# A selective-scan block and a dequantised projection on one core: the last operand of each half's sums moves to VectorE, the statistics are cut into pieces, and three engines get another order in a chunk's border pairs

## The chip, the core and the metric

The kernel runs on one core of a Trainium2 chip. A core has a matrix engine (TensorE, PE in the profile), a vector engine (VectorE, DVE), a scalar engine (ScalarE, ACT), a general one (GpSimd, POOL) and a DMA-issuing queue (SyncE, SP). Each runs its own instruction stream in program order, and they meet at semaphores. The metric is the device time of one execution in microseconds (us).

## What is computed

For 4096 rows of 1024 numbers:

```
n  = layernorm(x)                                   # eps 1e-5
xi, z = split(n @ in_proj_w)                        # 1024 -> 2 * 2048
xc = silu(conv_b + sum_k conv_w[k] * shift(xi, k))  # 4 taps along the rows
p  = xc @ x_proj_w.T                                # 64 + 16 + 16 columns
dt = softplus(rmsnorm(p[:64]) @ dt_proj_w.T + dt_bias);  B, C = rmsnorm(p[64:80]), rmsnorm(p[80:96])
h[t] = exp(dt[t] * A) * h[t-1] + dt[t] * B[t] * xc[t]      # 16 states for each of 2048 channels
y[t] = sum over the 16 states of h[t] * C[t]
x2 = x + ((y + D * xc) * silu(z)) @ out_proj_w.T
out = x2 + layernorm(x2) @ W.T + bias               # W = scale * (code - 128)
```

## The kernel before

**Tiling.** The rows are cut into 16 chunks (c) of T = 256. The 2048 channels are 16 tiles of 128 partitions, taken two at a time: 8 pairs (j = 0 to 7). One step handles pair j of chunk c, S = 8c + j, so there are 128 steps. Beside the scan of chunk c a step holds one eighth of four other stages: the input projection, convolution and x-projection of chunk c+1, the output projection of chunk c-1 and the dequantised projection (ffn) of chunk c-2. Once in a chunk, around its border, two groups of 16 transposes of normalised rows are made: those of chunk c+2 for the input projection (`norm1`, last pair, j = 7) and those of chunk c-2 for the ffn (`norm2`, first pair, j = 0). Each is a chain: VectorE takes `bn_stats` of four blocks and `bn_aggr`, ScalarE turns them into a scale and a shift and writes two normalised row blocks into `xrow`, TensorE transposes four groups of four, and ScalarE copies each group out of PSUM.

**The scan of a pair.** A step has 16 units (two states each). For a unit ScalarE keeps the last state (`copy`, L1057) and writes two exponentials (L1061) into a PSUM bank `hb`; GpSimd has written dt * B * x for four states into `dbx` (L486); VectorE runs the scan in place (`scan(u)`, L1342) and multiplies by C (`product(u)`, L1290). GpSimd then adds the two halves of each pair of products (`half`, L494, eight groups k = 0 to 7 in a step), and TensorE sums the two remaining operands of each group into a PSUM bank by multiplying with the identity (`group(k)`, L574, two matmuls of 256 columns each). Groups 0 to 3 go to the bank `ys0` (channel tile a = 0), groups 4 to 7 to `ys1` (a = 1). When a tile's four groups are in, VectorE multiplies by the gate (`y_gate`, L1301) and raises `y_ready`. The gate of tile 0 stands after `product(9)` of its own step; that of tile 1 is called `late_y` and stands in the next step, after `product(1)`.

**What shares the banks.** `ys1` also receives the x-projection (`x_proj`, L604) and the dt projection (L624): `x_proj` in step S waits for `y_ready` of tile 1 of step S-1 (2S of them). `ys0` also receives the z projection (L614), whose second half waits for tile 0's gate. `g1` takes the output projection (L767, in four parts, `out_proj(0)` to `(3)`) and the ffn (L689) in turn, each behind VectorE's addition of the other (L1272: `add_out`, `add_ffn`). `gx` takes the input projection (L594) and all border transposes (L581).

**What sets the order.** Nothing is scheduled by a planner: every engine's order in a step is the order in which the code calls its pieces. On TensorE a middle pair is ffn, groups 6 and 7 of the step before, out(0), x_proj, out(1), group 0, x_in(0), group 1, x_in(1), group 2, out(2), group 3, dt, out(3), z(1), group 4, z(0), group 5.

Of the kernel before, what the change touches and what calls it, by code (L numbers as in the profile page):

```python
# [86 lines left out]
def build_program(nc, x, win, wout, wf_codes, wf_scales, ffn_bias, xproj, dtw_in, convw_in, convb_in,  # L87
                  alog_in, dparam_in, lnw_in, out):
    ctx = ExitStack()
    with ctx:  # L90
# [14 lines left out]
        def dsem(name):  # L105
# [108 lines left out]
        conv, scans, hcs, y_ready = sem("conv"), sem("scans"), sem("hcs"), sem("y_ready")  # L214
        xp_add, o_add, f_add = sem("xp_add"), sem("o_add"), sem("f_add")
        rms_red, l1_dve, l1_stats, l2_dve, l2_stats, aggr_go = (sem("rms_red"), sem("l1_dve"), sem("l1_stats"),
                                                                sem("l2_dve"), sem("l2_stats"), sem("aggr_go"))
# [226 lines left out]
        def _(pool):  # L444
# [122 lines left out]
        def _(pe):  # L567
            def group_sum(SG, k):
# [4 lines left out]
                for i in range(2):  # L573
                    mm = nc.tensor.matmul(ys[a][:, 0:T], ident[:], half[:, k % 4, i * T:(i + 1) * T],  # L574
                                          start=False, stop=(q == NQ - 1 and i == 1), skip_group_check=True)
# [87 lines left out]
            def iteration(st, c):  # L663
                def step(j):
# [52 lines left out]
                    def norm2(i):  # L717
                        if not (first and st.ffn):
                            return
# [71 lines left out]
                    if first and st.ffn or last and st.norm1:  # L791
# [10 lines left out]
                        norm1(3)  # L802
                    else:
                        out_proj(0)
                        x_proj()
                    out_proj(1)
                    if not (first and st.ffn or last and st.norm1):
                        group(0)
# [5 lines left out]
                    out_proj(2)  # L814
                    group(3)
                    dt_proj()
# [72 lines left out]
        def _(act):  # L889
# [144 lines left out]
            def iteration(st, c):  # L1034
                def step(j):
# [72 lines left out]
                    def norm2(i):  # L1108
                        if first and st.ffn:
                            if i == 0:  # L1110
                                act.wait_ge(f_mm, after(PAIRS * (c - 2)))
                            norm_evac(x2nT, 4 * (c - 2), i, gx, l2_tr, l2_evac)
# [47 lines left out]
                    norm2(0)  # L1160
                    norm1(0)
                    unit(4)
                    first_skip_term()
                    norm2(1)
                    norm1(1)
                    unit(5)
                    norm2(2)
                    norm1(2)
                    unit(6)
                    norm2(3)  # L1170
                    norm1(3)
                    unit(7)
                    rms_square()
                    unit(8)
                    rms_apply()
                    unit(9)
                    unit(10)
                    unit(11)
                    ss_out()
                    unit(12)  # L1180
                    x_taps()
# [5 lines left out]
                    norm1_start()  # L1187
                    norm1_row(0)
                    unit(15)
                    norm1_row(1)  # L1190
# [23 lines left out]
        def _(dve):  # L1214
            def stats(rows, bst, mv, mid, done, n):
                for tt in range(TT):
                    for h in range(2):
                        ins = nc.vector.bn_stats(bst[:, tt, 6 * h:6 * h + 6], rows(tt, h))  # L1218
                ins.then_inc(mid, 1)
                dve.wait_ge(mid, after(n))  # L1220
                dve.sem_inc(aggr_go, 1)
# [3 lines left out]

            def norm1_stats(chunk):
# [289 lines left out]
```

## Time and profile before

| what | value |
|---|---|
| median of 3 runs | 4703.04 us (4701.97 to 4705.4) |
| the profiled execution | 4697.21 us |
| its span, from the first to the last instruction | 4695.4 us |
| first scan / first scan of the last pair, from the span's start | 128.08 / 4535.14 us |
| PE, DVE, POOL, ACT busy, share of the span | 95%, 89%, 86%, 75% |
| a steady chunk (chunks 3 to 13) | 279.55 to 279.90 us |

A step's length is taken here from one `scan(0)` on VectorE to the next one. In chunk 8 the eight steps are, by these starts, 40.16, 33.20, 33.20, 33.20, 33.20, 33.20, 34.43 and 39.29 us. The idle time in square brackets in a row of the timeline is the engine's time without work just before the row, with the instruction that ended it.

### The profile page before, as it was taken

The numbers are of one execution on the slowest core, as the hardware profiler recorded it, in microseconds if no ns is written. First come the engines' busy times: TensorE is split into PE (matmuls) and PEld (weight loads), VectorE is DVE, ScalarE is ACT, GpSimd is POOL, SyncE is SP. The second block draws the span as 40 slices with busy tenths as digits, with TensorE's granted clock in tenths as the row PEclk, the third lists the DMA queues.
The fourth block names the chain that finished last, engine by engine and source line by source line (L and its number), as shares of the span: only waits on it lengthen the run. The fifth ranks groups of instructions, "written<-read, shape, count | busy, mean of one in ns | idle before, by whom it ended". The sixth has DMA issues, their size and how long they took to land.

```text
span 4695.4 us, 80181 instructions
## 1 busy us (share of the span) xinstructions
PE 4448.9 (95%) x26656; PEld 4049.0 (86%) x26656; DVE 4160.0 (89%) x5745; ACT 3542.4 (75%) x8848; POOL 4039.2 (86%) x2942
## 2 busy tenths in 40 slices
PE   7788989999999999999999999999999999999889
PEld 6567879989898998989989898998989889898779
DVE  3898989989899998989989899998989989899981
ACT  3777787877778787777877878787787777778760
POOL 0898989989898998989989898998989899899990
PEclk9889999999999999999999999999999999999999
DMA  7324243353434435343353534334353443434232
GB/s 255 130 79 161 99 159 139 114 186 133 173 129 161 145 138 175 124 178 128 123 188 123 177 137 165 137 128 173 138 180 120 145 165 129 165 127 155 90 115 94
DMA packets 160285, 678.56 MB, mean 145 GB/s; under 512 B 21120, under 2 KB 30080, under 8 KB 110720
## 3 DMA queue, kind: packets, MB, share of 16 engines
q1 hardware_dynamic: 141440, 639.88, 39.0%
q10 hardware_dynamic: 18432, 33.56, 1.9%
q8 instruction: 212, 3.47, 0.3%
q14 instruction: 201, 1.65, 0.1%
HBM read 618.32 MB, written 55.05 MB: 143 GB/s over the span
## 4 chain that ended last, share of the span: by engine, by line
PE 59%; DVE 20%; POOL 7%; issue 6%; ACT 5%; DMA 1%; SPq 0%; DVEq 0%; POOLq 0%; ACTq 0%
PE g L767 13%; PE gx L594 13%; PE ys L574 12%; DVE hb L1342 11%; PE ys L614 9%; PE g L689 4%; POOL dbx L486 4%; DVE hc L1290 4%; DVE gx L1238 2%; POOL half L494 2%; PE ys L604 2%; DVE bst L1218 2%; PE gx L581 2%; ACT hb L1061 1%; PE hb L853 1%
## 5 line engine op out<-in xcount | busy, mean ns | idle before, releaser
L1342 DVE TENSOR_TENSOR_SCAN hb<-hb,dbx 128x512 f32<-128x512 f32 x2048 | 2498.0, 1220 | 108.0 <-ACT hb L1061 84.4
L486 POOL TENSOR_TENSOR dbx<-dtx,bb 128x1024 f32<-128x1024 f32 x1024 | 2421.0, 2364 | 60.1 <-DVE hb L1342 34.9
L1061 ACT ACTIVATE hb<-dt,a_neg 128x256 f32<-128x256 f32 x4096 | 1789.5, 468 | 66.3
L494 POOL TENSOR_TENSOR half<-hc 128x512 f32<-128x512 f32 x1024 | 1303.1, 1273 | 135.4 <-DVE hc L1290 120.4
L1290 DVE TENSOR_TENSOR hc<-hb,cb 128x512 f32<-128x512 f32 x2048 | 1378.9, 673 | 0.0
L574 PE MATMUL ys<-half,ident 128*128 128x256 f32 x4096 | 1073.2, 389 | 133.4 <-POOL half L494 119.2
L574 PEld LDWEIGHTS ys<-half,ident 128*128 128x128 f32 x4096 | 757.2, 194 | 254.3 <-POOL half L494 151.3
L767 PEld LDWEIGHTS g<-wo,ybuf 128*128 128x128 f32 x7680 | 954.0, 198 | 20.2 <-issue 1.3
L767 PE MATMUL g<-wo,ybuf 128*128 128x128 f32 x7680 | 966.7, 281 | 0.6 <-issue 0.6
L614 PE MATMUL ys<-xnT,wz 128*128 128x256 f32 x4096 | 928.8, 380 | 1.6 <-DVE ybuf L1301 1.6
L594 PE MATMUL gx<-xnT,wx 128*128 128x256 f32 x3968 | 904.5, 381 | 4.3 <-DMA wx<-in_win 2.6
L1057 ACT COPY hstate<-hb 128x2 f32<-128x2 f32 x2044 | 319.3, 156 | 757.7 <-DVE hc L1290 754.5
L614 PEld LDWEIGHTS ys<-xnT,wz 128*128 128x128 f32 x4096 | 770.6, 191 | 103.1 <-DVE ybuf L1301 2.8
L594 PEld LDWEIGHTS gx<-xnT,wx 128*128 128x128 f32 x3968 | 756.9, 192 | 108.5 <-DMA wx<-in_win 3.0
L689 PEld LDWEIGHTS g<-wf,x2nT 128*128 128x128 f32 x3552 | 414.1, 192 | 5.7
L689 PE MATMUL g<-wf,x2nT 128*128 128x128 f32 x3552 | 414.5, 275 | 0.0
L1301 DVE TENSOR_TENSOR ybuf<-ys,gate 128x256 f32<-128x256 f32 x256 | 107.0, 418 | 237.8 <-PE ys L574 237.6
L1238 DVE SCALAR_TENSOR_TENSOR gx<-xpre,convw,gx 128x256 f32<-128x256 f32 x744 | 302.0, 482 | 13.8 <-ACT gx L942 13.8
L512 POOL TENSOR_TENSOR dtx<-dt,xcs 128x2 f32<-128x2 f32 x128 | 25.3, 198 | 282.7 <-ACT dt L992 176.8
L604 PE MATMUL ys<-xprojw,xcn 128*128 128x96 f32 x1024 | 152.0, 298 | 26.6 <-ACT xcn L951 23.5
L604 PEld LDWEIGHTS ys<-xprojw,xcn 128*128 128x128 f32 x1024 | 143.2, 215 | 33.9 <-issue 21.5
L1067 ACT ACT_TABLE_LOAD x128 | 164.2, 1283 | 2.3
(105 smaller groups left out, 2766.1 us busy)
## 6 DMA issues: line engine op xcount, KB each, us to landing
wz<-in_win SPq DMA_DIRECT2D x128, 1024.0 KB, 4.8
wx<-in_win SPq DMA_DIRECT2D x124, 1024.0 KB, 4.8
wo<-in_wout SPq DMA_DIRECT2D x123, 1024.0 KB, 4.9
wf<-wf_scratch SPq DMA_DIRECT2D x113, 512.0 KB, 3.2
xc_scratch<-xcn ACTq DMA_DIRECT2D x128, 256.0 KB, 2.1
xcs<-xc_scratch SPq DMA_DIRECT2D x128, 256.0 KB, 5.0
bb<-bc_scratch SPq DMA_DIRECT2D x64, 512.0 KB, 7.5
cb<-bc_scratch SPq DMA_DIRECT2D x64, 512.0 KB, 6.7
```

The lines of the kernel that those rows point to most:

```text
L486: nc.gpsimd.tensor_tensor(dbx[:, k % 2, :].rearrange("p (n t) -> p n t", n=NQ), dtx[:, S % 2, a, :].unsqueeze(1).to_broadcast([P, NQ, T]), ...
L494: nc.gpsimd.tensor_tensor(half[:, k % 4, :], hc[:, k % 2, 0:HALF], hc[:, k % 2, HALF:GW], ALU.add).then_inc(halves, 1)
L574: mm = nc.tensor.matmul(ys[a][:, 0:T], ident[:], half[:, k % 4, i * T:(i + 1) * T], start=False, stop=(q == NQ - 1 and i == 1), skip_group ...
L594: mm = nc.tensor.matmul(pair_bank(q)[:, a * T:(a + 1) * T], pair_weights(q)[:, kk, a * P:(a + 1) * P], xnT[:, chunk % 2, kk, :], start=(kk ...
L604: mm = nc.tensor.matmul(ys[1][:, tt * E:(tt + 1) * E], xcn[:, a * T + tt * P:a * T + (tt + 1) * P], xprojw[:, 2 * (q % PAIRS) + a, :], sta ...
L614: mm = nc.tensor.matmul(ys[0][:, a * T:(a + 1) * T], wz[:, kk, a * P:(a + 1) * P], xnT[:, q // PAIRS % 2, kk, :], start=(kk == 0), stop=(k ...
L689: mm = nc.tensor.matmul(g1[:, tt * P:(tt + 1) * P], x2nT[:, kk, tt * P:(tt + 1) * P], wf[:, kk, :], start=(kk == 0), stop=(kk == KH - 1))
L767: mm = nc.tensor.matmul(g1[:, tt * P:(tt + 1) * P], ybuf[:, (1 - st.parity) * PAIRS + kt // 2, (kt % 2) * T + tt * P:(kt % 2) * T + (tt + ...
L1061: ins = nc.scalar.activation(h[:, m * T:(m + 1) * T], dt[:, j % 2, a, :], ACT.Exp, scale=a_neg[:, ds((2 * j + a) * N + 2 * v + m, 1)])
L1238: nc.vector.scalar_tensor_tensor(bank[:, a * T:(a + 1) * T], xpre[:, a, tap:tap + T], convw[:, ds((2 * jq + a) * KC + tap, 1)], bank[:, a ...
L1290: nc.vector.tensor_tensor(hc[:, k % 2, w * UW:(w + 1) * UW], hb[u % 4][:], cb[:, n:n + 2, :].rearrange("p n t -> p (n t)"), ALU.mult).then ...
L1342: nc.vector.tensor_tensor_scan(h[:], h[:], dbx[:, k % 2, w * UW:(w + 1) * UW], 0.0, ALU.mult, ALU.add).then_inc(scans, 1)
```

## The change

- **The last operand of a half.** TensorE's groups 3 and 7 have one matmul in place of two. A new VectorE step, `last_sum`, adds the other operand from SBUF onto the PSUM bank, and the gate waits for it (semaphore `summed`). It waits for the group's matmul. GpSimd waits for `y_ready` before it writes groups 3 and 7 anew.
- **Where VectorE has the gates.** `late_sum` stands where `late_y` stood, and `late_y` is behind `scan(3)`. Likewise for tile 0: `last_sum` stands where the gate stood and the gate is behind `scan(11)`; in the last pair `last_sum` is behind `scan(12)` and the gate behind `product(11)`.
- **Statistics in pieces.** One `bn_stats` for `norm1` in each of pairs 1 to 4, with `bn_aggr` in pair 5; for `norm2` one each in pairs 5 and 6 and two in pair 7, with `bn_aggr` there. Before: four and `bn_aggr` in pair 6, and four and `bn_aggr` in pair 7.
- **The first pair.** TensorE does all of the output projection first, then the transposes, in `gx` and `g1` by turns, the dt projection, group 3 and the whole input projection. ScalarE writes the two normalised row blocks after units 5 and 6 and copies the transposes out before units 8 to 11; its work on the convolution (`x_taps`) stands after unit 14. VectorE's `add_out` stands after `product(7)` and its taps after `product(13)`.
- **Pairs 6 and 7.** ScalarE normalises the rows of `norm1` after units 8 to 10 of pair 6 (before: after units 14 and 15). TensorE has group 3 ahead of out(2) in pair 7.

VectorE around the gate of tile 1 in a middle pair, before (`SCALAR_TENSOR_TENSOR hb` is a scan, `hc` a product, `x2<-g1` is `add_ffn`, `ybuf<-ys1` is `late_y`):

```order
L1272 TENSOR_TENSOR x2<-g1,x2 128x2x128
L1342 SCALAR_TENSOR_TENSOR hb2<-hb2,dbx 128x512
L1290 TENSOR_TENSOR hc<-hb1,cb 128x512
L1301 TENSOR_TENSOR ybuf<-ys1,gate 128x256
L1342 SCALAR_TENSOR_TENSOR hb3<-hb3,dbx 128x512
L1290 TENSOR_TENSOR hc<-hb2,cb 128x512
```

The same place now, where `ys1<-ys1,half` is the new sum:

```order
L1310 TENSOR_TENSOR x2<-g1,x2 128x2x128
L1392 SCALAR_TENSOR_TENSOR hb2<-hb2,dbx 128x512
L1332 TENSOR_TENSOR hc<-hb1,cb 128x512
L1341 TENSOR_TENSOR ys1<-ys1,half 128x256
L1392 SCALAR_TENSOR_TENSOR hb3<-hb3,dbx 128x512
L1351 TENSOR_TENSOR ybuf<-ys1,gate 128x256
L1332 TENSOR_TENSOR hc<-hb2,cb 128x512
```

One instruction is new, and the gate of tile 1 is one scan and one sum later in the row.

TensorE in the first pair before, behind groups 6 and 7 (`ys0` or `ys1<-half` are groups, `gx<-ident` transposes, `g1<-wo` the output projection, `ys1<-xprojw` x_proj, `gx<-xnT` x_in, `ys1<-ssmT` dt):

```order
L581 MATMUL gx<-ident,xrow 128x128 x4
L604 MATMUL ys1<-xprojw,xcn 128x96 x4
L581 MATMUL gx<-ident,xrow 128x128 x4
L767 MATMUL g1<-wo,ybuf 128x128 x8
L581 MATMUL gx<-ident,xrow 128x128 x4
L574 MATMUL ys0<-half,ident 128x256 x2
L581 MATMUL gx<-ident,xrow 128x128 x4
L767 MATMUL g1<-wo,ybuf 128x128 x8
L594 MATMUL gx<-xnT,wx 128x256 x8
L574 MATMUL ys0<-half,ident 128x256 x2
L594 MATMUL gx<-xnT,wx 128x256 x8
```

The same stretch now, from x_proj on:

```order
L609 MATMUL ys1<-xprojw,xcn 128x96 x4
L773 MATMUL g1<-wo,ybuf 128x128 x8
L579 MATMUL ys0<-half,ident 128x256 x2
L773 MATMUL g1<-wo,ybuf 128x128 x8
L579 MATMUL ys0<-half,ident 128x256 x2
L773 MATMUL g1<-wo,ybuf 128x128 x8
L586 MATMUL gx<-ident,xrow 128x128 x4
L586 MATMUL g1<-ident,xrow 128x128 x4
L579 MATMUL ys0<-half,ident 128x256 x2
L586 MATMUL gx<-ident,xrow 128x128 x4
L586 MATMUL g1<-ident,xrow 128x128 x4
L629 MATMUL ys1<-ssmT,dtw 128x256 x2
```

The transposes moved behind all of the output projection and the input projection behind them.

The diff, cut to its core:

```diff
@@ POOL
             def group_sum(S, k):
                 pool.wait_ge(sum_mm, after(8 * S + k - 3))
+                if k % NQ == NQ - 1:
+                    pool.wait_ge(y_ready, after(2 * S + k // NQ))
@@ PE
             def group_sum(SG, k):
-                for i in range(2):
+                for i in range(1 if q == NQ - 1 else 2):
...
                     def norm2(i):
+                        pe.wait_ge(l2_ready, after(2 * (c - 2) + i // 2 + 1))
                         if i == 0:
                             pe.wait_ge(sx_act, after(xs_done))
-                            pe.wait_ge(l2_ready, after(2 * (c - 1)))
-                        else:
-                            pe.wait_ge(l2_evac, after(4 * (c - 2) + i))
-                        transposes(xrow, i, gx, l2_tr)
+                        if i == 1:
+                            pe.wait_ge(o_add, after(S - PAIRS + 1))
+                        if i >= 2:
+                            pe.wait_ge(l2_evac, after(4 * (c - 2) + i - 1))
+                        transposes(xrow, i, (gx, g1)[i % 2], l2_tr)
@@ ACT, a step
+                    unit(2)
                     norm2_start()
-                    norm2_row(0)
-                    unit(2)
-                    norm2_row(1)
                     unit(3)
                     silus()
-                    norm2(0)
-                    norm1(0)
                     unit(4)
                     first_skip_term()
-                    norm2(1)
+                    norm1(0)
+                    unit(5)
+                    norm2_row(0)
                     norm1(1)
-                    unit(5)
-                    norm2(2)
+                    unit(6)
+                    norm2_row(1)
                     norm1(2)
-                    unit(6)
-                    norm2(3)
+                    unit(7)
+                    norm2(0)
                     norm1(3)
-                    unit(7)
                     rms_square()
                     unit(8)
+                    norm2(1)
                     rms_apply()
+                    norm1_start()
                     unit(9)
+                    norm2(2)
+                    norm1_row(0)
                     unit(10)
+                    norm2(3)
+                    norm1_row(1)
                     unit(11)
...
@@ DVE
+            def norm1_piece(chunk, i):
+                tt, h = divmod(i, 2)
+                dve.wait_ge(xrow_in, landed(chunk + 1))
+                dve.wait_ge(l1_stats, after(chunk))
+                nc.vector.bn_stats(bst1[:, tt, 6 * h:6 * h + 6], xrow[:, tt, h * 512:(h + 1) * 512]).then_inc(l1_dve, 1)
...
+            def last_sum(SP, a):
+                k = NQ * (a + 1) - 1
+                dve.wait_ge(sum_mm, after(8 * SP + k + 1))
+                dve.wait_ge(halves, after(8 * SP + k + 1))
+                nc.vector.tensor_tensor(ys[a][:, 0:T], ys[a][:, 0:T], half[:, k % 4, T:HALF], ALU.add
+                                        ).then_inc(summed, 1)
             def y_gate(SP, a):
-                dve.wait_ge(sum_mm, after(8 * SP + NQ * (a + 1)))
+                dve.wait_ge(summed, after(2 * SP + a + 1))
...
+                    def norm_stats():
+                        if st.norm1 and 1 <= j <= 4:
+                            norm1_piece(c + 2, j - 1)
+                        if st.norm1 and j == 5:
+                            norm1_aggregate(c + 2)
+                        if st.outproj and j in (5, 6):
+                            norm2_piece(c - 1, j - 5, 0)
+                        if st.outproj and last:
+                            norm2_piece(c - 1, 0, 1)
+                            norm2_piece(c - 1, 1, 1)
+                            norm2_aggregate(c - 1)
...
                     product(1)
+                    late_sum()
+                    scan(3)
                     late_y()
-                    scan(3)
                     product(2)
...
                     product(9)
-                    y_gate(S, 0)
+                    if not (last and st.norm1):
+                        last_sum(S, 0)
                     scan(11)
+                    if not (last and st.norm1):
+                        y_gate(S, 0)
                     product(10)
```

## Rows read from the trace of the kernel before

**Rows 1.** The page: the chain that ended last, shares by engine.

```profile
PE 59%; DVE 20%; POOL 7%; issue 6%; ACT 5%; DMA 1%; SPq 0%; DVEq 0%; POOLq 0%; ACTq 0%
```

**Rows 2.** Windows: chunk 8, its pairs 3, 6, 7, then pair 0, chunk 14.

```profile
core 0: us, PE busy (x) PEld busy (x) DVE busy (x) ACT busy (x) POOL busy (x), PEclk, DMA share, GB/s
...
2355.22:2635.11 279.89, 273.34 (x1668) 250.57 (x1668) 258.63 (x359) 220.92 (x554) 252.48 (x184) 0.99 0.43 149
...
2461.79:2494.99 33.20, 33.20 (x206) 30.61 (x206) 31.60 (x44) 26.04 (x65) 30.86 (x23) 1.00 0.38 130
...
2561.39:2595.82 34.43, 34.43 (x217) 31.84 (x217) 34.12 (x50) 29.22 (x72) 32.15 (x24) 1.00 0.38 132
...
2595.82:2635.11 39.29, 37.75 (x239) 33.93 (x239) 34.72 (x52) 30.81 (x83) 30.89 (x24) 1.00 0.47 160
...
2635.11:2675.28 40.17, 35.17 (x196) 31.73 (x196) 31.80 (x45) 30.72 (x74) 32.76 (x26) 0.92 0.66 235
...
4034.57:4307.73 273.16, 263.73 (x1601) 242.04 (x1601) 253.77 (x347) 213.96 (x538) 252.40 (x184) 0.98 0.40 141
```

**Rows 3.** Timeline, PE, middle pair: start, us, what (each matmul is two passes).

```profile
2466.57 1.95 PE L767 MATMUL g<-wo,ybuf 128*128 128x128 f32 x16
2468.35 1.03 PE L604 MATMUL ys<-xprojw,xcn 128*128 128x96 f32 x8
...
2482.32 1.03 PE L574 MATMUL ys<-half,ident 128*128 128x256 f32 x4
...
2485.83 3.62 PE L614 MATMUL ys<-xnT,wz 128*128 128x256 f32 x16
```

**Rows 4.** Timeline, DVE, the same pair.

```profile
2465.22 0.41 DVE L1272 TENSOR_TENSOR x<-g,x 128x256 f32<-128x256 f32 x1
...
2467.27 0.41 DVE L1301 TENSOR_TENSOR ybuf<-ys,gate 128x256 f32<-128x256 f32 x1
2467.60 1.22 DVE L1342 TENSOR_TENSOR_SCAN hb<-hb,dbx 128x512 f32<-128x512 f32 x1
2468.73 0.67 DVE L1290 TENSOR_TENSOR hc<-hb,cb 128x512 f32<-128x512 f32 x1
...
2483.38 0.42 DVE L1301 TENSOR_TENSOR ybuf<-ys,gate 128x256 f32<-128x256 f32 x1 [1.43 <-PE ys L574]
```

**Rows 5.** Groups: line, operation, shapes, count | busy, mean ns | idle before.

```profile
L1061 ACT ACTIVATE hb<-dt,a_neg 128x256 f32<-128x256 f32 x4096 | 1789.5, 468 | 66.3
...
L1238 DVE SCALAR_TENSOR_TENSOR gx<-xpre,convw,gx 128x256 f32<-128x256 f32 x744 | 302.0, 482 | 13.8 <-ACT gx L942 13.8
...
L994 ACT ACT_TABLE_LOAD x128 | 164.2, 1283 | 2.3
...
L1272 DVE TENSOR_TENSOR x<-g,x 128x256 f32<-128x256 f32 x240 | 98.7, 411 | 35.8 <-PE g L838 29.6 <-PE g L689 6.2
...
L909 ACT ACTIVATE xrow<-x,nmr,rstd 128x1024 f32<-128x1024 f32 x32 | 39.3, 1233 | 0.5
```

**Rows 6.** Timeline, PE: chunk 1, pair 7 of chunk 8, pair 0 of chunk 9.

```profile
503.76 1.53 PE L574 MATMUL ys<-half,ident 128*128 128x256 f32 x4 [2.41 <-POOL half L494]
505.08 3.23 PE L767 MATMUL g<-wo,ybuf 128*128 128x128 f32 x16
...
2601.17 0.66 PE L581 MATMUL gx<-ident,xrow 128*128 128x128 f32 x4 [0.90 <-ACT xcn L951]
...
2638.72 1.13 PE L574 MATMUL ys<-half,ident 128*128 128x256 f32 x4 [2.42 <-POOL half L494]
2642.43 1.12 PE L581 MATMUL gx<-ident,xrow 128*128 128x128 f32 x4 [2.58 <-ACT xcn L951]
```

**Rows 7.** Timeline, DVE: pair 6 and 7 of chunk 8, pair 0 of chunk 9.

```profile
2579.74 2.46 DVE L1218 BATCH_NORM_STATS2 bst<-xrow 128x6 f32<-128x512 f32 x4
...
2620.61 0.42 DVE L1301 TENSOR_TENSOR ybuf<-ys,gate 128x256 f32<-128x256 f32 x1 [3.74 <-PE ys L574]
...
2663.67 0.42 DVE L1301 TENSOR_TENSOR ybuf<-ys,gate 128x256 f32<-128x256 f32 x1 [4.07 <-PE ys L574]
```

More of the change, by code:

```diff
@@ L790, in step @@
                     late_group(7)
[L791 to L793 removed]
+                    if first and st.ffn:
+                        out_proj(0)
+                        x_proj()
+                        out_proj(1)
+                        group(0)
+                        out_proj(2)
+                        group(1)
+                        out_proj(3)
+                        norm2(0)
+                        norm2(1)
+                        group(2)
+                        norm2(2)
+                        norm2(3)
+                        dt_proj()
+                        group(3)
+                        x_in_proj(0)
+                        x_in_proj(1)
+                        z_in_proj(1)
+                        group(4)
+                        z_in_proj(0)
+                        group(5)
+                        return
+                    norm1(0)
+                    if last and st.norm1:
                         x_proj()
[L795 removed]
                         norm1(1)
                         out_proj(0)
[L798 removed]
                         norm1(2)
                         group(0)
[L801 removed]
                         norm1(3)
+                        out_proj(1)
                     else:
@@ L805, in step @@
                         x_proj()
-                    out_proj(1)
-                    if not (first and st.ffn or last and st.norm1):
+                        out_proj(1)
                         group(0)
@@ L813, in step @@
                     group(2)
-                    out_proj(2)
-                    group(3)
-                    dt_proj()
+                    if last and st.norm1:
+                        group(3)
+                        out_proj(2)
+                        dt_proj()
+                    else:
+                        out_proj(2)
+                        group(3)
+                        dt_proj()
                     out_proj(3)
@@ L1180, in step @@
                     unit(12)
-                    x_taps()
+                    if not (first and st.ffn):
+                        x_taps()
                     dt_softplus()
@@ L1186, in step @@
                     unit(14)
-                    norm1_start()
-                    norm1_row(0)
+                    if first and st.ffn:
+                        x_taps()
                     unit(15)
-                    norm1_row(1)
                 steps(c, step)
@@ L1214, in _, with aggregate @@
         def _(dve):
[L1215 to L1221, printed above, removed]
+            def aggregate(bst, mv, mid, done, n):
+                dve.wait_ge(mid, after(4 * n))
                 for tt in range(TT):
@@ L1352, in late_product, with late_sum @@
                             times_c(S - 1, UNITS - 1)
+                    def late_sum():
+                        if was.scan and not (first and c == 0):
+                            last_sum(S - 1, 1)
                     def late_y():
@@ L1415, in step @@
                     product(7)
+                    if first and st.ffn:
+                        add_out()
                     scan(9)
                     product(8)
-                    if pre and st.norm1:
-                        norm1_stats(c + 2)
                     scan(10)
                     product(9)
-                    y_gate(S, 0)
+                    if not (last and st.norm1):
+                        last_sum(S, 0)
                     scan(11)
+                    if not (last and st.norm1):
+                        y_gate(S, 0)
                     product(10)
                     scan(12)
+                    if last and st.norm1:
+                        last_sum(S, 0)
                     product(11)
-                    taps()
+                    if last and st.norm1:
+                        y_gate(S, 0)
+                    if not (first and st.ffn):
+                        taps()
                     scan(13)
                     product(12)
-                    add_out()
-                    norm2_stats()
+                    if not (first and st.ffn):
+                        add_out()
+                    norm_stats()
                     scan(14)
                     product(13)
+                    if first and st.ffn:
+                        taps()
                     scan(15)
```

49 lines of the change are left out of this document (27 added, 22 removed).

## The prediction

> **What bounds the kernel now.** I read the page's chain first: 59% of it is TensorE and 20% VectorE [rows 1]. Then the busy time in windows that hold one pair each, since the border pairs differ from the rest [rows 2]. In a middle pair (1 to 5) TensorE is busy all 33.20 us of the 33.20; VectorE has 31.60, GpSimd 30.86. Pair 6 is VectorE's, 34.12 of 34.43. In pair 7 and the next chunk's pair 0 neither is full: 39.29 us with 37.75 and 34.72, 40.17 us with 35.17 and 31.80. Last I followed single instructions in a middle pair on both engines, because the change moves instructions across a loop of waits: VectorE's gate of tile 1 (`late_y`) releases TensorE's x_proj, and TensorE's group 3 releases VectorE's tile 0 work, which stands ahead of the next `late_y`.
>
> The length of that loop decides. Before: from tile 0's gate at 2483.38 VectorE runs without a gap to the next pair's `late_y`, whose end by the period is 2467.27 + 0.41 + 33.20 = 2500.88: 17.50 us [rows 4]. TensorE runs from x_proj's start, 2468.35, to group 3's end, 2483.35, without a gap: 15.00 us [rows 3]. Together 32.50 in a period of 33.20. The slack is visible: `late_y` ends at 2467.68, x_proj starts 0.67 later because TensorE is still at work. So the loop is just hidden behind TensorE.
>
> **Prices.** One identity matmul of 256 columns is half of group 3: 1.03 us for two holds the last pass's tail; by the starts around a group, two cost 0.86, one 0.43. VectorE's rows start before the one ahead is written back, so I count start to start: 0.33 for a 128x256 sum that reads PSUM (2467.27 to 2467.60 for the gate), 1.13 for a scan (2467.60 to 2468.73) [rows 4], about 0.60 for one statistic (2.46 us for four [rows 7]). `last_sum` writes PSUM and has no row of its own. It lies between the 0.33 of a sum into SBUF and the 0.39 by which the taps (L1238, PSUM to PSUM, 0.48 busy [rows 5]) follow each other; I take 0.35, near the sum because it is the same operation. Ends 0.33 and 0.39 move a pair by 0.08 at most.
>
> The Trainium skill, "VectorE: DVE Perf Modes", section "The TRN2 errata", charges a PSUM source 120 cycles beside one for each element, at 0.96 GHz; an estimate from it is 0.39 us. The trace has 0.33 for the gate's sum and 0.39 only where the result also goes to PSUM. By the page's price the total below would be some 8 us longer.
>
> **Middle pairs.** TensorE saves 2 x 0.43: 33.20 - 0.86 = 32.34. VectorE rises to 31.60 + 0.70 + 0.60 (a statistic in pairs 1 to 4) = 32.9. GpSimd's 30.9 and its new waits are no bound: the gates they ask for stand some ten us ahead. But the loop changes too. TensorE's part loses one matmul, -0.43. VectorE's part gains `last_sum` of tile 0 (0.35), the statistic (0.60), `late_sum` (0.35), and the scan that now stands between `late_sum` and `late_y` (1.13): 32.50 - 0.43 + 2.43 = 34.50. It is above every engine's own work, so a middle pair costs 34.5, +1.3. What is late is x_proj: nothing else on TensorE may pass it, and TensorE idles 34.5 - 32.34 = 2.2 us, most of it in front of x_proj. Behind it wait out(1), groups 0 to 3, the input projection, and VectorE's `last_sum`, some 1.9 us. Tile 0's gate behind scan(11) costs nothing: it comes 0.35 + 1.13 + 0.42 = 1.9 behind group 3, and z(1) starts 2.5 behind it [rows 3]. Pair 5 has also the two aggregates (0.36): 34.9.
>
> **Pair 6.** The four statistics with their aggregates go (2.8), one comes (0.6), two sums (0.7): VectorE 34.12 - 1.5 = 32.6. The loop holds it at 34.5, +0.1. ScalarE's normalisation here is hidden, since units 8 to 11 are some 2 us early.
>
> **Pair 7.** TensorE's x_proj waits for `late_y` at 7.4, the transposes are interleaved as before, and by the durations above group 3 ends at 23.9 and dt at 26.5 into the pair. VectorE no longer stops 3.74 us for group 3 [rows 7], since scans 11 and 12 are ahead of the sum. But the softplus needs dt, and its table load (1.28 [rows 5]) and unit 13's exponentials follow: scan(13) starts at 29.65 where VectorE is at 28.1. Work 34.72 + 0.70 - 1.20 (two statistics fewer) = 34.2, waits 1.55 there, 0.65 for the squares, 0.4 at scan(9): 36.8, against 39.29: -2.5.
>
> **Pair 0.** The gain seems large: the trace's 2.42 and 2.58 of idle TensorE [rows 6] and 4.07 of idle VectorE at group 3 [rows 7] go. Others take their place. x_proj starts at 7.7, and behind it come out(1), group 0, out(2), group 1, out(3): the first transposes end at 16.3. ScalarE has their copy ahead of unit 8, so scan(8) starts at 18.0 instead of 15.6 (2.4). The second transposes write `g1` and wait for `add_out`, which stands behind `product(7)` and ends at 20.1: TensorE idles 4 us. Their copy stands ahead of unit 9: scan(9) at 23.05 instead of 20.05 (3.0). Then 0.4 at scan(10), about 1.1 at scans 13 and 14 behind softplus, and 0.7 in small ones (`add_ffn`, scans 4 and 7, taps). 31.80 + 0.70 + 7.6 = 40.1 with the overlapped tails counted twice; walking by starts I get 39.7. So -0.5. And x_in waits for the last copy at 25.6; two x_in, two z_in (3.45 each), two groups and the ffn (3.57) follow, to 44.9, which is 5.2 into pair 1, where `add_ffn` stands at 3.4 [rows 4]. Pair 1: 34.5 + 1.9 = 36.4.
>
> **Sum for a chunk:** 39.7 + 36.4 + 3 x 34.5 + 34.9 + 34.5 + 36.8 = 285.8, against 279.9 [rows 2]: +5.9. Twelve such chunks (2 to 13): +71. Chunk 14 has no norm1 and runs 273.16 [rows 2]: its middle pairs go to 33.9, pairs 5 and 6 to 34.5, pair 7 to 35.6, in all +8.6. Chunk 1, without the ffn, already has TensorE waiting (34.33 a pair); it gains in pair 7: -2. Chunk 0, chunk 15 (no x_proj, so no loop) and the tail: 0. Total +78: 4697.2 + 78 = 4775 for a profiled execution. The median before is 5.8 above the profiled one, so 4781 for the median.
>
> **Rivals.**
>
> *TensorE's clock falls in the middle pairs.* The granted clock fell to 1.2 GHz after 2.41 us without work in chunk 1, and after 2.42 and 2.58 in pair 0, not after 0.90 in pair 7 [rows 6], where it is 1.00 of the full one [rows 2]. At the low level group 7 and out(0) took 1.53 and 3.23 instead of 1.03 and 1.95: +1.8 us. My idle time of 2.2 a pair is in pieces (about 0.1, 0.25, 1.7), below those. If it falls in each pair behind x_proj, it lies in the loop: 1.7 x 6 pairs x 12 = +120, 4900. For it: pair 5 and pair 0 come near. Against it: the longest piece is 1.7.
>
> *The other side: the loop doesn't close.* If x_proj came in time, as the slack of 0.67 now suggests, a pair would cost the largest of 32.34, 32.9 and 30.9: -0.3 in pairs 1 to 4, 0 in 5, -1.5 in 6, -2.5 in 7, and pair 0 some 37 for 40.2: -7.4 a chunk, in 13 chunks -96, about 4605. It needs `late_y` to end before 6.3 into the pair. By the order it ends at 7.4, and it decides once the loop's added time is below 1.1 instead of 2.0. What speaks for it: the scan's place is all that closes it, and the border pairs have over 12 us to give.
>
> The Trainium skill, "Perfetto Trace Analysis", section "Identifying the Most-Contended Engine", has one improve first the engine with the highest occupancy; that is TensorE here, and this rival is what the rule gives. The trace agrees on who is full in a middle pair, not that nothing stands next: the loop is 0.7 behind.
>
> *The borders pay for it.* If pair 0 came to 37.5 and left nothing to pair 1, a chunk would be 281.7, +1.8: 4727. If pair 7 also reached 34.9, it would be level: 4703. It would need ScalarE's copies not to hold units 8 and 9.
>
> **Chances.** Forecast 68%, its own range 4725 to 4830; clock 17%, 4830 to 4920; loop open 10%, 4590 to 4690; borders level 5%, 4690 to 4725. Range for 8 in 10: 4712 to 4880. A measurement of this kernel tells 0.2%, 9 us. Slower 0.86, same 0.03, faster 0.11.
>
> **What would show it.** In middle pairs: x_proj idle before it, released by VectorE's gate, about 1.7 us; idle VectorE at `last_sum` of tile 0, about 1.9, released by TensorE; scan(0) to scan(0) 34.5. Pair 6 34.5, pair 7 near 37 with its wait at scan(13). Pair 0: TensorE idle some 4 us ahead of the transposes in `g1`, VectorE idle at scans 8 and 9 behind ScalarE, `add_ffn` of pair 1 late. A sum into PSUM by 0.33 to 0.39. It is wrong if x_proj follows out(0) without a gap, if middle pairs are below 33.2, or if pair 0 is below 37.

## The result and the profile after

The changed kernel takes 4865.58 us (median of 4 runs, 4858.22 to 4874.56), the one before 4702.51 on the same chip (4701.74 to 4705.4). The ratio is 1.0346, with a 95% interval of 1.0328 to 1.0364: 3.5% slower, where the forecast said 1.7% slower. The direction was right and the time lies in the range for 8 in 10 (4712 to 4880), but 85 us above the forecast of 4781 and above its own range (to 4830): 163 us were added where 78 were forecast.

The lengths of the steps, by the starts of `scan(0)`, mean over chunks 3 to 13 (us; the last column is the median of the runs):

| kernel | pair 0 | 1 | 2 to 4 | 5 | 6 | 7 | chunk | median |
|---|---|---|---|---|---|---|---|---|
| before | 40.11 | 33.20 | 33.20 | 33.20 | 34.43 | 39.29 | 279.83 | 4702.5 |
| forecast | 39.7 | 36.4 | 34.5 | 34.9 | 34.5 | 36.8 | 285.8 | 4781 |
| after | 43.36 | 36.99 | 34.63 | 34.77 | 34.63 | 38.50 | 292.15 | 4865.6 |

Pairs 2 to 6 are as forecast, to 0.13 us. The miss is in the border pairs. I read the windows first: chunk 10's middle pair 3, pair 7 of chunk 9, pairs 0 and 1 of chunk 10 (columns as in [rows 2]):

```profile
3105.62:3140.25 34.63, 33.08 (x202) 29.77 (x201) 32.76 (x47) 26.03 (x65) 32.08 (x24) 1.00 0.36 125
2985.37:3023.45 38.08, 35.19 (x207) 31.61 (x206) 34.31 (x53) 30.32 (x80) 29.63 (x22) 0.96 0.39 130
3023.45:3068.51 45.06, 38.46 (x209) 34.77 (x208) 32.84 (x47) 30.93 (x76) 34.00 (x28) 0.85 0.62 237
3068.51:3105.62 37.11, 36.10 (x224) 33.17 (x223) 32.85 (x47) 26.25 (x65) 30.82 (x23) 1.00 0.39 127
```

In the middle pair no engine fills the period any more: the largest is TensorE with 33.08 of 34.63, where it had 33.20 of 33.20. In pair 0 the granted clock is 0.85 of full (0.92 before), and TensorE's busy time is 38.46 (35.17 before, with 196 passes in the window where there are 209 now: part of the rise is work of pair 7 that falls into this window). In pair 7 the granted clock is 0.96, where it was 1.00.

**The loop.** TensorE and VectorE in that middle pair, which answer to [rows 3] and [rows 4]:

```profile
3107.74 1.03 PE L579 MATMUL ys<-half,ident 128*128 128x256 f32 x4
3108.93 0.70 PE L579 MATMUL ys<-half,ident 128*128 128x256 f32 x2 [0.16 <-POOL half L498]
...
3113.02 1.13 PE L609 MATMUL ys<-xprojw,xcn 128*128 128x96 f32 x8 [1.39 <-DVE ybuf L1351]
...
3127.08 0.60 PE L579 MATMUL ys<-half,ident 128*128 128x256 f32 x2
```

```profile
3111.10 0.42 DVE L1341 TENSOR_TENSOR ys<-ys,half 128x256 f32<-128x256 f32 x1
3111.43 1.22 DVE L1392 TENSOR_TENSOR_SCAN hb<-hb,dbx 128x512 f32<-128x512 f32 x1
3112.56 0.40 DVE L1351 TENSOR_TENSOR ybuf<-ys,gate 128x256 f32<-128x256 f32 x1
...
3127.72 0.43 DVE L1341 TENSOR_TENSOR ys<-ys,half 128x256 f32<-128x256 f32 x1 [1.87 <-PE ys L579]
```

Both waits that the forecast named are there: x_proj waits 1.39 for VectorE's gate (forecast about 1.7), and `last_sum` waits 1.87 for TensorE (about 1.9). The loop has no slack left: x_proj's start to group 3's end is 14.66, `last_sum` of tile 0 to the next `late_y`'s end (3112.56 + 0.40 + 34.63 = 3147.59) is 19.87, and the two handovers are 0.04 and 0.06. The sum is 34.63; it must be, as the period itself is used for the next `late_y`. What the rows show is how small the handovers are: before, x_proj started 0.67 after `late_y`'s end.

**Pair 0 of chunk 10**, TensorE, ScalarE and VectorE (at 45.06 us one of the two longest; chunks 3 to 13 range from 40.90 to 45.06, mean 43.36):

```profile
3028.32 0.70 PE L579 MATMUL ys<-half,ident 128*128 128x256 f32 x2 [0.22 <-POOL half L498]
3031.37 3.75 PE L773 MATMUL g<-wo,ybuf 128*128 128x128 f32 x16 [2.35 <-issue]
3034.92 1.86 PE L609 MATMUL ys<-xprojw,xcn 128*128 128x96 f32 x8
3036.57 2.37 PE L773 MATMUL g<-wo,ybuf 128*128 128x128 f32 x16
...
3044.08 0.60 PE L586 MATMUL gx<-ident,xrow 128*128 128x128 f32 x4
3048.71 1.08 PE L586 MATMUL g<-ident,xrow 128*128 128x128 f32 x4 [4.03 <-DVE x L1310]
```

```profile
3044.77 0.59 ACT L955 COPY x2nT<-gx 128x512 f32<-128x512 f32 x1 [7.58 <-PE gx L586]
3049.84 0.59 ACT L955 COPY x2nT<-g 128x512 f32<-128x512 f32 x1 [3.51 <-PE g L586]
```

```profile
3030.87 0.40 DVE L1351 TENSOR_TENSOR ybuf<-ys,gate 128x256 f32<-128x256 f32 x1
...
3046.43 1.23 DVE L1392 TENSOR_TENSOR_SCAN hb<-hb,dbx 128x512 f32<-128x512 f32 x1 [5.82 <-ACT hb L1090]
...
3051.42 1.23 DVE L1392 TENSOR_TENSOR_SCAN hb<-hb,dbx 128x512 f32<-128x512 f32 x1 [2.85 <-ACT hb L1090]
```

Here is what the forecast had not seen. It let out(0) run before `late_y` and x_proj behind it. But in the first pair the code has `if first: pe.wait_ge(y_ready, after(2*c*PAIRS))` in `out_proj`: out(0) reads what `late_y` writes, so it waits as x_proj does. The row puts the wait down to "issue"; the gate, VectorE's first row here, ends at 3031.27 and out(0) starts at 3031.37. So out(0) starts 7.9 us into the pair, with x_proj behind it, and TensorE has idled 2.35 us in one piece. Then both run at the low clock: out(0) 3.75 instead of 1.95, x_proj 1.86 instead of 1.03. The first transposes end at 21.2 us (forecast 16.3), ScalarE's copy holds unit 8, and VectorE waits 5.82 at scan(8), not 2.4. The 4.03 for `add_out` was forecast as 4.

The same place in chunk 8, whose pair 0 starts at 2440.47 and takes 40.90:

```profile
2445.55 0.70 PE L579 MATMUL ys<-half,ident 128*128 128x256 f32 x2 [0.77 <-POOL half L498]
2448.26 2.02 PE L773 MATMUL g<-wo,ybuf 128*128 128x128 f32 x16 [2.02 <-issue]
2450.12 1.03 PE L609 MATMUL ys<-xprojw,xcn 128*128 128x96 f32 x8
...
2458.10 0.60 PE L586 MATMUL gx<-ident,xrow 128*128 128x128 f32 x4
```

Out(0) waits here too, but runs at the full clock, and the first transposes end at 18.2. So the two effects come apart in one trace. In chunks 3 to 13 the wait ahead of out(0) is 2.02 us (2.35 in chunk 10 alone), and out(0) takes 2.02 in chunks 5, 6, 8 and 13 and 3.29 to 3.76 in the other seven.

**Pair 7 of chunk 9:**

```profile
2988.68 0.70 PE L579 MATMUL ys<-half,ident 128*128 128x256 f32 x2 [0.15 <-POOL half L498]
2990.72 0.66 PE L586 MATMUL gx<-ident,xrow 128*128 128x128 f32 x4 [1.34 <-ACT xcn L980]
2992.77 1.82 PE L609 MATMUL ys<-xprojw,xcn 128*128 128x96 f32 x8 [1.39 <-DVE ybuf L1351]
...
2995.23 2.53 PE L773 MATMUL g<-wo,ybuf 128*128 128x128 f32 x16
```

Three waits come close together, 0.15, 1.34 and 1.39, and x_proj and out(0) run at the low clock in whole or in part (1.82 and 2.53). Before, waits of 0.47, 0.90 and 0.17 stood there at the full clock, the second in [rows 6] and the other two here:

```profile
2599.14 1.13 PE L574 MATMUL ys<-half,ident 128*128 128x256 f32 x4 [0.47 <-POOL half L494]
...
2603.07 0.66 PE L581 MATMUL gx<-ident,xrow 128*128 128x128 f32 x4 [0.17 <-ACT xnT L926]
```

Over the span the waits behind this (who <- for whom: us in all, times, longest):

```profile
DVE ys L1341 <- PE ys L579: 180.1, 107, 4.8
PEld ys L609 <- DVE ybuf L1351: 160.7, 100, 3.2
DVE hb L1392 <- ACT hb L1090: 157.1, 88, 5.8
```

x_proj's wait stands in 100 steps. On the page, TensorE's share of the span falls from 95% to 91%, and its share of the chain that ended last rises from 59% [rows 1] to 66%. Its busy share says less than before of who sets the end: most of its work from x_proj to group 3 stands in the loop, whatever share of the period it fills.

### The profile page after: what moved, and what is told of

Same layout as the page of the kernel before. It is cut to its first block, busy times and chain, and to the rows that moved or that the text cites. A ratio compares the mean times of both kernels' runs of the same rounds, so it can differ in the third digit from the quotient of the medians.

```text
span 4872.7 us, 79820 instructions
## 1 busy us (share of the span) xinstructions
PE 4435.7 (91%) x26144; PEld 3986.4 (82%) x26144; DVE 4244.8 (87%) x6001; ACT 3539.2 (73%) x8848; POOL 4039.5 (83%) x2942
## 4 chain that ended last, share of the span: by engine, by line
PE 66%; DVE 13%; POOL 11%; issue 6%; DMA 3%; ACT 1%; SPq 1%; DVEq 0%; POOLq 0%; ACTq 0%
PE gx L599 17%; PE g L773 13%; PE ys L579 12%; PE ys L619 10%; POOL dbx L487 6%; DVE hb L1392 6%; PE g L694 5%; POOL half L498 4%; PE ys L609 3%; DVE hc L1332 3%; DVE gx L1276 2%; PE ys L629 1%; DMA b_scratch<-ssmT 1%; PE hb L882 1%; DVE ybuf L1351 1%
## 5 line engine op out<-in xcount | busy, mean ns | idle before, releaser
L579 PE MATMUL ys<-half,ident 128*128 128x256 f32 x3584 | 981.5, 394 | 120.0 <-POOL half L498 114.8
L773 PE MATMUL g<-wo,ybuf 128*128 128x128 f32 x7680 | 987.9, 284 | 31.4 <-issue 31.4
L579 PEld LDWEIGHTS ys<-half,ident 128*128 128x128 f32 x3584 | 658.0, 195 | 249.6 <-POOL half L498 171.1
L609 PE MATMUL ys<-xprojw,xcn 128*128 128x96 f32 x1024 | 165.8, 313 | 161.7 <-DVE ybuf L1351 138.2
L1341 DVE TENSOR_TENSOR ys<-ys,half 128x256 f32<-128x256 f32 x256 | 108.3, 423 | 180.6 <-PE ys L579 180.1
```

What stands on the lines that cost most here:

```text
L609: mm = nc.tensor.matmul(ys[1][:, tt * E:(tt + 1) * E], xcn[:, a * T + tt * P:a * T + (tt + 1) * P], xprojw[:, 2 * (q % PAIRS) + a, :], sta ...
L773: mm = nc.tensor.matmul(g1[:, tt * P:(tt + 1) * P], ybuf[:, (1 - st.parity) * PAIRS + kt // 2, (kt % 2) * T + tt * P:(kt % 2) * T + (tt + ...
```

## The experiments

Each was timed beside the kernel before; ratios carry a 95% interval.

**1 to 3. Three of the change's parts, each alone on the kernel before.** `a_only`: `last_sum`, the gates behind scans 3 and 11. `b_only`: the statistics in pieces. `c_only`: the first pair's order. The fourth part, the order of pairs 6 and 7, has no run of its own on this kernel.

```diff
 a_only, VectorE          |  b_only, VectorE
+late_sum()               | -norm1_stats(c + 2)   # pair 6
-late_y()                 | -norm2_stats()        # pair 7
 scan(3)                  | +norm_stats()         # in pairs 1 to 7
+late_y()                 |
```

> The kernel before with only the new sums: one matmul less in groups 3 and 7, last_sum on VectorE, the gates one scan later. Loop theory: the loop late_y, x_proj, group 3, last_sum is 32.50 - 0.43 + 0.70 + 1.13 = 33.9 us, so a middle pair is 33.9 against 33.20, x_proj waits for VectorE's gate, in all some 4765 to 4780 us. Rival (the sums are hidden, TensorE's saving counts): middle pairs at most 32.9, below 4700 us. Second rival (the clock falls behind x_proj's wait): middle pairs above 35.

> The kernel before with only the statistics in pieces. Loop theory: pairs 1 to 4 have a loop of 32.50 + 0.60 = 33.1 us, just under TensorE's 33.20, so they stay at 33.20; pair 5 33.2 to 33.5; pair 6 falls from 34.43 to 33.2 and pair 7 by about 1.2: some 4675 us, faster by 0.6%. Rival (statistics cost wherever they stand): middle pairs 33.8, no gain, 4700 us or more.

> The kernel before with only the first pair's new order on the three engines. Theory: in pair 0 out_proj(0) now waits for late_y (at 6 us into the pair, where it ends in this kernel), the transposes in g1 wait for add_out, and ScalarE's units 8 and 9 wait behind the copies: pair 0 about 41.5 us for 40.2 and pair 1 about 35.5 for 33.2, in all near 4750 us. Rival (the excess of pair 0 in the changed kernel comes only from the later gate and the fallen clock): pair 0 at most 38, the kernel at or below 4700 us.

| kernel | pair 0 | 1 | 2 to 4 | 5 | 6 | 7 | chunk | median | ratio |
|---|---|---|---|---|---|---|---|---|---|
| a_only | 39.87 | 34.04 | 34.04 | 34.04 | 34.83 | 41.64 | 286.54 | 4793.68 | 1.0197 (1.0180 to 1.0214) |
| b_only | 39.68 | 33.79 | 33.30 | 33.45 | 33.31 | 37.99 | 278.13 | 4683.53 | 0.9965 (0.9952 to 0.9978) |
| c_only | 41.24 | 35.88 | 33.20 | 33.20 | 34.43 | 39.29 | 283.64 | 4752.74 | 1.0113 (1.0098 to 1.0128) |

The before of these runs is 4700.4. By the forecast's prices the loop of a_only is 32.50 - 0.43 + 0.35 + 0.35 + 1.13 = 33.90; measured 34.04. Its median is 14 us above what was expected; pair 7, still in its old order, grew to 41.64, 28 us over twelve chunks. b_only came 9 us above what was expected and c_only where it was. In b_only's pair 1 (33.79) TensorE is busy all the time with 211 passes for 206, so the 0.59 there is carried work and not the statistic's price. The window of one of its middle pairs:

```profile
3054.00:3088.04 34.04, 32.65 (x202) 29.85 (x202) 32.16 (x47) 26.04 (x65) 32.08 (x24) 1.00 0.37 127
```

So a is +93 us, b -17, c +52: +128 of the +163. The other 35 come from the parts together and from the fourth part (experiment 6 splits them in two).

**4. late_y_first.** The changed kernel with the gate of tile 1 directly behind its sum.

```diff
 late_sum()
-scan(3)
 late_y()
+scan(3)
```

> The changed kernel with late_y moved back ahead of scan(3), directly behind late_sum. Loop theory: the loop loses 1.13 us of the scan and gains at most 0.1 for the wait between the two, so middle pairs go from 34.63 to 33.5 to 33.6 us, pairs 0 and 7 fall by 1 to 2 each, in all near 4750 us for 4866. Rival (VectorE's added work, not the place of the gate, sets the middle pair): they stay at 34.6.

Middle pairs 33.64, median 4768.93, ratio 1.0148 (1.0132 to 1.0163). The middle pair loses 0.99 of the scan's 1.13, x_proj's wait falls from 1.39 to 0.40:

```profile
3073.09 1.13 PE L609 MATMUL ys<-xprojw,xcn 128*128 128x96 f32 x8 [0.40 <-DVE ybuf L1351]
```

One scan's place is worth 97 us of the 163, with pair 0 (41.53) and pair 1 (35.81) also shorter. The theory of the loop stands. The expected time was some 20 us lower: pair 7, expected 1 to 2 us shorter, was 38.85 for 38.50.

**5. warm.** The changed kernel with matmuls of the identity that nobody reads, put into TensorE's waits at four places of pairs 0 and 7: 9 and 15 of them in pair 0, 4 and 5 in pair 7 (the first place is shown, without the waits that make the bank free).

```diff
+    idle_work(g1, 9)         # pair 0
     out_proj(0)
     x_proj()
```

> The changed kernel with idle matmuls (identity times identity, results unused) in TensorE's waits of the border pairs: 9 ahead of out_proj(0) and 15 ahead of the transposes in g1 in pair 0, 4 and 5 around the first transposes in pair 7; 0.22 us each, less than the waits they fill. Clock theory (the granted clock falls in those waits and the half-speed stretch lies on the path): pair 0 from 43.4 to about 40.3 us, pair 7 from 38.5 to about 37.1, in all near 4810 us for 4866. Rival (the excess over the forecast is the wait of out_proj(0) for late_y and the order of the waits alone): no change or a little longer, 4866 to 4880.

Median 4808.16, ratio 1.0229 (1.0213 to 1.0244); pair 0 40.56, pair 7 37.09, middle pairs 34.63. Pair 0 of chunk 9:

```profile
2991.82 2.17 PE L700 MATMUL g<-ident 128*128 128x128 f32 x18
2994.22 2.02 PE L778 MATMUL g<-wo,ybuf 128*128 128x128 f32 x16 [0.22 <-issue]
2996.08 1.03 PE L609 MATMUL ys<-xprojw,xcn 128*128 128x96 f32 x8
...
3004.06 0.60 PE L586 MATMUL gx<-ident,xrow 128*128 128x128 f32 x4
```

out(0) takes 2.02 instead of 3.75 and x_proj 1.03 instead of 1.86, behind the same wait for the gate. The low clock is worth 57 us, two thirds of the miss of 85. The first transposes start 17.8 us into the pair (which begins at 2986.29) and end at 18.4, as in chunk 8 of the changed kernel: out(0)'s own wait is what stays between that and 16.3.

**6. no_c.** The changed kernel with the first pair in its old order, on TensorE, ScalarE and VectorE.

> The changed kernel with pair 0 in the old order on TensorE, ScalarE and VectorE. The sums, the statistics in pieces and pair 7's order stay. Theory: pair 0 about 40 us for 43.4 and pair 1 34.6 for 37.0, middle pairs 34.63 as they are, in all near 4790 us. Rival (pair 0 is long because of the late gate, whatever the order): pair 0 at 42 or more.

Median 4793.44, ratio 1.0196 (1.0180 to 1.0211); pair 0 39.34, pair 1 34.63, pair 7 39.38, chunk 286.67. The first pair's order costs 72 us in the changed kernel and 52 alone. What is left, a, b and the order of pairs 6 and 7, costs 91, though 93 - 17 is 76. By the steps of the profiled executions, over chunks 2 to 13 against the sum of a_only and b_only: pairs 2 to 5 take 23 us more, as the statistic now lies in a loop that bounds; pair 6 takes 11 more, as the loop holds what b_only saved there; pair 7, which has its new order here, takes 14 less. That is 19 with pair 0's -1 for the medians' 15. The reasons given for pairs 2 to 6 follow from the loop; what the order of pairs 6 and 7 gives alone isn't shown. The two excesses, 15 and 20, are the 35 left open above.

**7. add_out_early.** `add_out` of the first pair ahead of scan(8).

```diff
-scan(8)
-product(7)
 add_out()
+scan(8)
+product(7)
```

> The changed kernel with add_out of pair 0 ahead of scan(8) instead of behind product(7). Theory (the transposes in g1 wait for add_out, which waits for unit 8, which waits behind ScalarE's first copy): the wait of 4 us ahead of them goes to under 0.5, pair 0 from 43.4 to 39 to 40 us, in all near 4815 us. Rival (x_proj's place or the clock sets pair 0): at most 1 us a chunk, above 4850.

Median 4828.44, ratio 1.0270 (1.0255 to 1.0285); pair 0 40.23. TensorE's wait for `add_out` falls from 56.5 us in all to 22.2:

```profile
PE g L586 <- DVE x L1310: 22.2, 14, 3.9
```

In chunk 10 it is still 2.29, where under 0.5 was expected, and the time is 13 us above what was expected. The edit gives back 37 of the order's 72 us; part of that is clock, as the time at the low level also fell, from 373 to 319 us.

**8. ffn_half.** Is TensorE's load the bound of a middle pair? This kernel leaves out half of the ffn's sum.

```diff
-for kk in range(KH):
+for kk in range(KH // 2):
```

> The changed kernel with half of the ffn's matmuls in the steps left out (the second half of the sum over 1024), so its output is not the reference's. It takes 1.79 us a pair from TensorE at a place outside the loop of late_y, x_proj, group 3 and last_sum. Loop theory: middle pairs stay at 34.6 (up to 36 if the longer idle time lets the clock fall inside the loop), pair 1 falls by up to 1.8. Rival (TensorE's load sets the pair): middle pairs 1.5 us or more shorter.

Median 4866.27, ratio 1.0348 (1.0331 to 1.0365): no change. Pairs 2, 3 and 4 are 35.04, 34.87 and 34.63, and pair 6 is 34.63. TensorE has 1.79 us less work in a pair and the pair is not shorter; the loop doesn't hold the ffn. Pair 1 is 1.8 shorter, as there TensorE is behind. Where a middle pair is longer the clock is below full, and out(0), behind a wait of 1.94 (0.16 in the changed kernel) and one group, is slow:

```profile
2552.05:2587.03 34.98, 32.71 (x186) 29.27 (x185) 32.76 (x47) 26.03 (x65) 30.85 (x23) 0.95 0.35 123
```

```profile
2555.35 0.70 PE L579 MATMUL ys<-half,ident 128*128 128x256 f32 x2 [1.94 <-POOL half L498]
2556.04 3.07 PE L773 MATMUL g<-wo,ybuf 128*128 128x128 f32 x16
```

**9 to 12. Towards a faster kernel, from b_only.** The before of these is 4699.32. `pieces_in_wait` puts the pieces of pairs 1 to 6 ahead of tile 0's gate, where VectorE waits for group 3 anyway (1.43 in [rows 4]). `pieces_early_rows` adds the changed kernel's pairs 6 and 7 (normalised rows early, group 3 ahead of out(2), the gate behind product(11)). `pieces_out_first` is `pieces_in_wait` with out(0) ahead of the first transposes in pair 0; `all_three` has both.

```diff
 product(9)
+early_pieces()
 y_gate(S, 0)
 scan(11)
...
-norm_stats()
+late_pieces()            # pair 7 only
```

> The kernel before with the statistics in pieces, and the pieces of pairs 1 to 6 ahead of the gate of tile 0, where VectorE waits 1.4 us for group 3, instead of behind add_out. No other part of the change. Loop theory: the piece is then outside the loop, pairs 1 to 5 go back from 33.3 to 33.8 to TensorE's 33.20: about 0.9 us a chunk less than with the pieces behind add_out (4683.5), some 4672 us. Rival (VectorE's added work counts wherever it stands): no difference, 4683.

> The kernel of pieces_in_wait with the changed kernel's pairs 6 and 7 as well: ScalarE normalises norm1's rows after units 8 to 10 of pair 6, TensorE has group 3 ahead of out_proj(2) in pair 7, VectorE the gate of tile 0 behind product(11) there. Theory: VectorE's 3.7 us of waiting for group 3 in pair 7 go and about 1.5 of them stay saved (scan(13) waits for softplus behind dt): pair 7 about 36.5 for 38.0, in all some 4652 us. Rival (the saving is given back in pair 0, which then waits longer at the head): no gain, 4672.

> The kernel of pieces_in_wait with out_proj(0) ahead of the first transposes in pair 0, where TensorE waits 2.6 us for ScalarE. It waits for late_y there, at 5.9 us into the pair. Theory: it fills the wait, pair 0 about 38.5 us for 39.7 and less time at the low clock, some 4655 us. Rival (the late gate holds it as it does in the changed kernel): no gain, 4672 or more.

> The three together: pieces in VectorE's wait, norm1's rows and group 3 early, out_proj(0) ahead of the first transposes. If the gains add, some 4635 us; if the head of pair 0 gives back what pair 7 saves, 4655 or more.

| kernel | pair 0 | 1 to 6 | 7 | chunk | median | ratio |
|---|---|---|---|---|---|---|
| pieces_in_wait | 39.24 | 33.20 | 37.99 | 276.43 | 4653.49 | 0.9903 (0.9889 to 0.9917) |
| pieces_early_rows | 38.14 | 33.20 | 35.95 | 273.29 | 4614.85 | 0.9822 (0.9808 to 0.9835) |
| pieces_out_first | 39.32 | 33.20 | 37.99 | 276.51 | 4655.63 | 0.9908 (0.9894 to 0.9922) |
| all_three | 38.49 | 33.20 | 35.82 | 273.51 | 4621.93 | 0.9835 (0.9821 to 0.9848) |

```profile
2953.09 0.68 DVE L1231 BATCH_NORM_STATS2 bst<-xrow 128x6 f32<-128x512 f32 x1
2954.61 0.42 DVE L1316 TENSOR_TENSOR ybuf<-ys,gate 128x256 f32<-128x256 f32 x1 [0.84 <-PE ys L574]
```

These two rows of `pieces_early_rows` show the statistic where VectorE waits, with 0.84 of the wait still left: in the middle pairs it costs nothing, against 0.10 in pairs 2 to 4 in b_only. Its windows of pair 7, pair 0 and a middle pair:

```profile
2825.86:2861.67 35.81, 35.23 (x219) 31.80 (x218) 33.53 (x51) 30.74 (x83) 30.02 (x22) 1.00 0.43 149
2861.67:2899.82 38.15, 36.24 (x227) 32.61 (x226) 31.78 (x45) 30.65 (x74) 33.77 (x28) 1.00 0.75 280
2933.02:2966.22 33.20, 33.20 (x206) 30.61 (x206) 32.20 (x46) 26.02 (x65) 32.08 (x24) 1.00 0.37 129
```

TensorE is full in the middle pair, and in the border pairs the clock stays at 1.00 (0.92 in pair 0 before [rows 2]). `pieces_early_rows` is the fastest kernel here, 1.8% below the one before, and it takes from the change all but `last_sum`, the gates moved behind a scan for it and the first pair's order, with the statistics in another place. Three of the four times missed what was expected: 4653 for 4672, 4615 for 4652, 4622 for 4635, all lower. `pieces_early_rows` gained in pair 0 too (38.14 for 39.24), where its rival saw a loss. The fourth, 4656 for 4655 of `pieces_out_first`, is luck: it was to come from a gain in pair 0, and pair 0 is 39.32 for 39.24. out(0) ahead of the transposes brought nothing in either form.

## Why the prediction came out as it did

**Middle pairs: right, by its own mechanism.** The loop of late_y, x_proj, group 3 and `last_sum` closes at 34.63, forecast 34.50. The 0.13 is 0.10 of handovers that the sum left out, +0.09 on TensorE's part and -0.06 on VectorE's. late_y_first (the scan's place, 0.99), a_only (34.04) and ffn_half (TensorE's work is not in it) show it. The rival "the loop doesn't close" fell. Its condition was mis-stated: it was to hold with less than 1.1 us added to the loop, but by the forecast's own terms 32.50 stays below VectorE's 32.9 only with less than 0.4, and late_y_first, with some 0.9 added, still has the loop as its bound (33.64, x_proj waiting 0.40). Its price has a slip too: -0.3 four times, -1.5, -2.5 and -3.2 make -8.4 a chunk, not -7.4, so some 4594 us. The rule of the Trainium skill's "Perfetto Trace Analysis", section "Identifying the Most-Contended Engine", to improve the engine with the highest occupancy first, would have spoken for that rival if TensorE is taken by its matmul time: it was full and got 0.86 us less work, and the pair grew by 1.43. The same section of the Trainium skill says that for TensorE matmul time is no good measure of headroom and has, beside the rate of arithmetic, the time of weight loads taken: that was 30.61, below VectorE's 31.60 [rows 2]. Neither number shows the loop.

**Pairs 5 and 6: right.** 34.77 for 34.9, and 34.63 for 34.5.

**The price of the new sum: right.** 3111.10 to 3111.43 is 0.33 start to start, for an operand and a result in PSUM. The Trainium skill's "VectorE: DVE Perf Modes", section "The TRN2 errata", gives 0.39 by an estimate from its figure; start to start the trace doesn't agree, and the measurement decides; the row's own time is 0.42. Where the result goes doesn't explain the 0.39 of the taps, then.

**Pair 0: the step that failed.** The prediction put it: "x_proj starts at 7.7, and behind it come out(1), group 0, out(2), group 1, out(3): the first transposes end at 16.3." Out(0) is missing from that list: it waits for `late_y` too. That puts 1.8 us of it behind the gate and leaves TensorE 2.02 to 2.35 us without work in one piece, behind which out(0) and x_proj ran at the low clock, in whole or in part, in seven of eleven chunks. Measured for the first transposes: 21.2 us in chunk 10, 18.2 in chunk 8 where the clock stayed up, 18.4 in warm. Pair 0 is 43.4 instead of 39.7: 44 us over twelve chunks, and 6 in chunk 15. Pair 1 is 37.0 for 36.4, 7 us (36.7 in warm); its term has a slip of 0.1, as 5.2 less 3.4 is 1.8.

**Pair 7: a term mis-sized.** The forecast had 36.8 with TensorE at full clock. It added its waits for VectorE and ScalarE one by one and never asked what three together do to the clock; x_proj and out(0) ran at the low clock in whole or in part and the pair took 38.5: 22 us over twelve chunks. Warm brings it to 37.09, so the working of the waits was good to 0.3.

**The clock rival: right kind, wrong place.** It was put in the middle pairs, whose pieces of 0.16 and 1.39 did not lower it in the changed kernel. It fell in pairs 7 and 0, which the forecast had priced at full clock, though it had been low in part of pair 0 before (0.92 [rows 2]), not of pair 7 (1.00). The measured 4866 lies in this rival's range, 4830 to 4920, for another reason than the rival gave.

**The rest.** Chunks 0 and 1 cost some 5 us each above the forecast, and chunk 15 cost 8 where 0 was forecast; the tail is 0 as forecast. Chunk 14's +8.7 for +8.6 is luck: its pair 0 is 42.1 and its pair 7 32.3, where the forecast's terms had 39.7 and 35.6, and the two misses nearly cancel. These terms come from one profiled execution, which is 9 us above the median: with 44 in pair 0, 7 in pair 1, 22 in pair 7, 5 in the middle pairs and 3 ahead of the first scan they make up the 99 us by which it lies above the forecast of 4775. By the medians the miss of 85 is 57 clock (warm) and 28 that stay in warm. Out(0)'s wait is only part of these 28: warm's pair 0 is still 0.9 above its forecast, its pair 1 0.3 and its pair 7 0.3, and the rest stands in the middle pairs and in the first and last chunks. It wasn't taken apart by a run.

## What to carry to other kernels

Where two engines release each other once a step, add up the loop, with every instruction that stands between a wait and the release behind it, and compare it with each engine's own work: one scan ahead of the gate cost 97 us here, while 1.79 us less work a pair on the fullest engine brought nothing. For each moved instruction read its own waits in the code, for the border case above all, before it is put on a time line. Put added work where the engine waits already: the same statistics gave 0.35% in one place and 1.0% in the other.

## What the runs showed of the hardware

TensorE's granted clock was at its low level (1.2 of 2.4 GHz) for 261 us of the execution before, 373 after, 182 in warm and 545 in ffn_half, by the clock records of the traces; the mean granted clocks are 0.972, 0.962, 0.981 and 0.944.

The longest single wait doesn't tell whether it falls. In pair 0 of chunks 3 to 13 the wait ahead of out(0) was 2.02 us in ten chunks, and out(0) ran at the full clock in four of them (2.02 us) and was slower in six (3.29 to 3.76). In add_out_early one out(0) behind 2.62 us kept the full clock (chunk 10), and in ffn_half one behind 1.94 us, with a group of 0.70 between, took 3.07. In pair 7 the clock fell with waits of 0.15, 1.34 and 1.39 us and some 0.7 us of matmuls between them; it stayed up with 0.16 and 1.39 in middle pairs, which have 2.7 us of matmuls between. What decides in pair 0 isn't shown.

In ffn_half, with 1.79 us of matmuls fewer in a pair, the clock was low in middle pairs too: leaving out work made other work slower. Matmuls that nobody reads, 1.2 to 3.5 us of them in a wait, kept it up in chunks 3 to 13 and gave back 57 us.

A sum of 128x256 on VectorE that reads PSUM took 0.33 us start to start, whether its result went to SBUF (the gate before, 2467.27 to 2467.60) or to PSUM (`last_sum`, 3111.10 to 3111.43).
